# In the attentions of a two-layer decoder, ScalarE copies a finished group's output ahead of that step's transposed probabilities

## The chip, the cores and the metric

The kernel runs on one core of one Trainium2 chip. The metric is the device time of one execution in microseconds (us), as the median of several runs. The core's engines are TensorE (PE in the profile; its weight loads are PEld), VectorE (DVE), ScalarE (ACT), GpSimd (POOL) and SyncE (SP). Each works through its own list of instructions in order, and they wait for each other on semaphores.

## The reference, cut to what matters

The program computes two decoder layers over 64 sequences of 128 tokens and 256 features. Layer 0 is a gated delta-rule recurrence, a cross attention with tanh projections, and a mixture of four experts. Layer 1 is a causal attention with one shared head of keys and values, a causal cross attention, and a mixture of eight experts. The change concerns the three softmax attentions, each with 16 heads of 16 features:

```python
scores = jnp.einsum('bqhd,bkhd->bhqk', qh, kh) * scale
attn = jax.nn.softmax(scores, axis=-1)
ctx = jnp.einsum('bhqk,bkhd->bqhd', attn, vh).reshape(b, s, D)
return ctx @ Wo + bo
```

The two attentions of layer 1 add a causal mask to the scores.

## The kernel before

The 64 sequences are taken four at a time: one iteration handles G = 4 sequences, and a hardware loop runs 16 iterations. Each iteration runs the delta rule, attention 0, mixture 0, attention 1, attention 2 and mixture 1. No scheduler is involved: every engine has its own list, written by hand, and the order of the code is the order on the engine.

**An attention** (`attention(a_no)` exists once on PE, once on ACT, once on DVE) works on 16 "quads" (`QUADS`): a quad is four heads of one sequence, so four quads make one sequence, here called a group. The three copies of the loop run over steps `u` from 0 to 23, and each engine does in step u the work of several quads at different stages:

- PE multiplies queries by keys for two quads (L1076, in even steps; in attentions 1 and 2 two further matmuls add the mask, L1082); transposes the probabilities of quad u-3 into bank 3 or 4 (L1090, signals `t_psum`); multiplies values by the transposed probabilities of quad u-4 into bank 5 (L1102, signals `pv`). One step after a group's copy-out it transposes the group's output (L1111, `otr_psum`), and a step later the normalised output (L1132). From step 20 on it multiplies by the output weights (L1124).
- DVE takes each quad's row maximum (L1775) and subtracts it (L1779, `s_sub`). Per group it divides the output by the sum (L1793 reciprocal, L1795 product, `o_norm`).
- ACT exponentiates quad u-2 (L739 in attention 0, L737 in the others, `p_exp`), copies the transposed probabilities of quad u-3 from PSUM to SBUF (L746, waits for `t_psum`, signals `pt`), and per group copies the finished output from bank 5 (L750, waits for `pv`, signals `o_sb`) and later the transposed normalised output (L754).

**The wait around bank 5.** All four quads of a group write quarters of bank 5. So before the first quad of the next group (quads 4, 8 and 12, in steps 8, 12 and 16) PE waits:

```python
if v % 4 == 0 and g > 0:
    pe.wait_ge(S["o_sb"], at(it, "o_sb", a_no * G + g))
```

ACT makes that copy (L750) in the same steps 8, 12, 16 and, for the last group, 20. Step 20 has no copy of probabilities.

**GpSimd beside the attentions.** From mixture 0 on POOL runs a long serial chain of small additions for the next iteration's decay gates (`chain_links`, `chain_products`, L567), started by the gate weights of mixture 0 (`g_w`, DVE L1891). It ends with `au` (L610, `au_ready`) and goes on with `centered(it, 1)`, whose last operation is a subtraction over the whole 128x1024 tile `x_in` (L501). DVE uses `au` inside attention 2: before the division of group 2 it runs parts 0 to 4 of `decay_exponential` (17 dependent small steps, L1474 to L1493, the first of which waits for `au_ready`), and before that of group 3 parts 5 to 9 (17 more, L1492 to L1510):

```python
if a_no == 2 and b >= 2:
    for part in range(5 * (b - 2), 5 * (b - 1)):
        decay_exponential(part)
```

Of the kernel before, what the change touches and what calls it, by code (L numbers as in the profile page):

```python
# [13 lines left out]
ACT = mybir.ActivationFunctionType  # L14
# [8 lines left out]
G = 4  # L23
# [4 lines left out]
QUADS = G * NH // QH  # L28
# [43 lines left out]
def decoder_kernel(nc, a, out):  # L72
# [7 lines left out]
    with ExitStack() as ctx:  # L80
# [3 lines left out]
        def sem(name):  # L84
            return ctx.enter_context(nc.semaphore(name))
# [59 lines left out]
        def cut(first, *shape):  # L145

            size = 1
            for n in shape:
                size *= n
            flat = arena[:, first * G * D:first * G * D + size]  # L150
            names = "abcde"[:len(shape)]
            return flat.rearrange(f"p ({' '.join(names)}) -> p {' '.join(names)}", **dict(zip(names, shape)))
# [53 lines left out]
        osb = cut(10, 2, N)  # L206
# [54 lines left out]
        bank = [ctx.enter_context(nc.psum_tensor(f"bank{n}", [P, 512], F32)) for n in range(8)]  # L261

        S = {name: sem(name) for name in PER}
# [6 lines left out]
        def nth(it, per, n, ahead=0):  # L270

            return it * per + (ahead * per + n)

        def at(it, name, n):

            assert n > 0
            return nth(it, PER[name], n)
# [340 lines left out]
        def _(act):  # L618
# [61 lines left out]
            with nc.Fori(0, NIT, engines=[act.engine], hint_back_edge=True) as it:  # L680
# [48 lines left out]
                def attention(a_no):  # L729
                    for u in range(QUADS + 8):  # L730
                        if u >= 2 and u - 2 < QUADS:
                            v = u - 2
                            act.wait_ge(S["s_sub"], at(it, "s_sub", a_no * QUADS + v + 1))
                            if a_no > 0:
                                if v == 0:
                                    act.wait_ge(S["hl_fix"], at(it, "hl_fix", 6 * (a_no + 2) + 6))
                                act.activation(Ssb[:, v % 4], Ssb[:, v % 4], ACT.Exp, scale=rstd[:, v // 4:v // 4 + 1]).then_inc(S["p_exp"], 1)  # L737
                            else:
                                act.activation(Ssb[:, v % 4], Ssb[:, v % 4], ACT.Exp, scale=SCALE).then_inc(S["p_exp"], 1)  # L739
                        if u >= 3 and u - 3 < QUADS:  # L740
                            v = u - 3
                            act.wait_ge(S["t_psum"], at(it, "t_psum", a_no * QUADS + v + 1))
                            if v >= 2:

                                act.wait_ge(S["pv"], at(it, "pv", a_no * QUADS + v - 1))
                            act.activation(PT[:, v % 2], bank[3 + v % 2][:, :].rearrange("p (h q) -> p h q", h=QH), ACT.Copy).then_inc(S["pt"], 1)  # L746
                        if u >= 5 and (u - 5) % 4 == 3 and (u - 5) // 4 < G:
                            b = (u - 5) // 4
                            act.wait_ge(S["pv"], at(it, "pv", a_no * QUADS + 4 * b + 4))
                            act.activation(osb[:, b % 2, :], bank[5][:, :], ACT.Copy).then_inc(S["o_sb"], 1)  # L750
                        if u >= 7 and (u - 7) % 4 == 3 and (u - 7) // 4 < G:
                            b = (u - 7) // 4
                            act.wait_ge(S["attT_psum"], at(it, "attT_psum", a_no * G + b + 1))
                            act.activation(attT[:, :, b * P:(b + 1) * P],  # L754
                                           bank[7][:, 0:C * P].rearrange("p (c t) -> p c t", c=C), ACT.Copy).then_inc(S["attT"], 1)
# [28 lines left out]
                for c in range(C):  # L784
                    key_masks(0, c, bank[6 + c], True)
                act.preload_act_table_set(LN_EXP_TABLE)
                attention(0)


# [33 lines left out]
                act.activation(latT, bank[2][:, :], ACT.Copy).then_inc(S["lat"], 1)  # L823
                latent_masks()
                attention(1)


                key_masks(2, 0, bank[2], False)
                xT_copy(4)
                key_masks(2, 1, bank[3], False)  # L830
                half_rstd(4)
                attention(2)


# [1219 lines left out]
```

## Time and profile before

| | us |
|---|---|
| median of 3 runs | 5632.31 (5630.9 to 5637.03) |
| profiled execution, whole | 5640.22 |
| its span | 5637.7 |
| PE busy | 4736.9 (84%) |
| DVE busy | 4265.8 (76%) |
| POOL busy | 3826.9 (68%) |
| ACT busy | 2325.5 (41%) |

Busy time is the sum over an engine's instructions, and the span runs from the first to the last of them. The chain that ended last puts 58% of the span on PE, 23% on DVE and 8% on ACT. TensorE's granted clock is near full after the first slices. One iteration takes about 331 us, and the three attentions lie at 389 to 426, 516 to 556 and 568 to 609 us in the first.

### The profile page before, as it was taken

Reading aid. Unit: us, or ns where it says so; the run is one execution under the profiler, and the core shown is the slowest. Engines: PE = TensorE matmul, PEld = TensorE weight load, DVE = VectorE, ACT = ScalarE, POOL = GpSimd, SP = SyncE. Lnnn points to the kernel's source line nnn. Section 1 sums busy time; section 2 is a strip of 40 time slices with the busy share of each in tenths; the row PEclk is TensorE's granted clock in tenths of the full one; section 3 lists DMA queues with packets and bytes.
Section 4 is the critical chain, followed back from the end, with each engine's and each line's share of the span. In section 5 each row is a group of like instructions: output and inputs, shape, how many; then the busy total and the mean of one; then the engine's idle time right before and its main releaser. Section 6 shows DMA issues by size and latency. Waiting matters only on the chain.

```text
span 5637.7 us, 105981 instructions
## 1 busy us (share of the span) xinstructions
PE 4736.9 (84%) x28362; PEld 3112.3 (55%) x28362; DVE 4265.8 (76%) x11558; ACT 2325.5 (41%) x4480; POOL 3826.9 (68%) x10625
## 2 busy tenths in 40 slices
PE   1069898888889889888988988898898889889888
PEld 0045655656566465655646565565656556565655
DVE  5868777777777778777777878777787877778777
ACT  0034344444334444444444444444443444444344
POOL 1158676785867678586767858676785867768585
PEclk7589999999999999999999999999999999999999
DMA  3000000000000000000000000000000000000000
GB/s 85 8 12 1 28 1 13 16 9 20 1 24 5 11 18 9 20 1 24 5 9 20 9 20 1 24 5 9 20 5 24 1 24 5 9 20 1 20 1 16
DMA packets 61879, 78.07 MB, mean 14 GB/s; under 512 B 11168, under 2 KB 53808, under 8 KB 61232
## 3 DMA queue, kind: packets, MB, share of 16 engines
q1 hardware_dynamic: 52784, 62.42, 3.4%
q10 hardware_dynamic: 8448, 8.39, 0.4%
q8 instruction: 240, 3.93, 0.3%
q14 instruction: 407, 3.33, 0.2%
HBM read 45.04 MB, written 8.46 MB: 9 GB/s over the span
## 4 chain that ended last, share of the span: by engine, by line
PE 58%; DVE 23%; issue 8%; ACT 8%; POOL 1%; SPq 1%; DMA 1%; DVEq 0%; ACTq 0%; POOLq 0%
PE bank L1171 8%; PE bank L1090 6%; PE bank L1204 5%; PE bank L1076 5%; PE bank L1102 4%; PE bank L1000 3%; PE bank L1124 3%; PE bank L1007 3%; PE bank L1189 2%; PE bank L1111 2%; DVE arena L2004 2%; PE bank L1082 2%; ACT arena L763 2%; ACT arena L750 1%; PE bank L1132 1%
## 5 line engine op out<-in xcount | busy, mean ns | idle before, releaser
L746 ACT ACTIVATE arena<-bank 128x512 f32<-128x512 f32 x768 | 454.4, 592 | 386.9 <-PE bank L1090 386.9
L1775 DVE TENSOR_REDUCE smax<-bank 128x4 f32<-128x512 f32 x768 | 525.5, 684 | 114.6 <-PE bank L1082 66.1
L1779 DVE TENSOR_TENSOR arena<-bank,smax 128x512 f32<-128x512 f32 x768 | 531.2, 692 | 26.4
L1090 PE MATMUL bank<-ident,arena 128*128 128x128 f32 x3072 | 489.4, 282 | 46.9 <-ACT arena L737 29.2
L1171 PE MATMUL bank<-w,arena 128*128 128x512 f32 x1024 | 482.2, 601 | 14.0 <-DVE arena L1727 14.0
L1102 PE MATMUL bank<-arena 128*32 128x128 f32 x6144 | 329.1, 286 | 192.3 <-ACT arena L750 192.3
L1076 PE MATMUL bank<-arena 64*128 64x512 f32 x1536 | 436.4, 645 | 64.4 <-ACT arena L774 28.0
L1090 PEld LDWEIGHTS bank<-ident,arena 128*128 128x128 f32 x3072 | 348.7, 142 | 247.8 <-ACT arena L739 83.0
L1204 PE MATMUL bank<-w,arena 128*128 128x256 f32 x2048 | 454.1, 380 | 13.9 <-ACT arena L809 13.9
L737 ACT ACTIVATE arena<-arena,rstd 128x512 f32<-128x512 f32 x512 | 368.2, 719 | 203.4 <-DVE arena L1779 197.5
L1204 PEld LDWEIGHTS bank<-w,arena 128*128 128x128 f32 x2048 | 387.8, 190 | 90.3 <-issue 23.0
L567 POOL TENSOR_TENSOR acc_a<-acc_s,arena 128x32 f32<-128x32 f32 x1008 | 262.7, 261 | 204.2 <-DVE gate L1891 80.5
L501 POOL TENSOR_TENSOR arena<-arena 128x1024 f32<-128x1024 f32 x17 | 32.2, 1896 | 517.1 <-DVE y_nat L1559 517.0
L809 ACT ACTIVATE arena<-bank,lnb,lng 128x512 f32<-128x512 f32 x256 | 197.1, 776 | 407.2 <-PE bank L1189 404.5
L567 POOL TENSOR_TENSOR acc_c<-acc_a,acc_b 128x32 f32<-128x32 f32 x1008 | 267.1, 265 | 79.7
L567 POOL TENSOR_TENSOR acc_s<-acc_a,acc_c 128x32 f32<-128x32 f32 x1008 | 265.3, 263 | 78.9
L567 POOL TENSOR_TENSOR acc_c<-acc_c,arena 128x32 f32<-128x32 f32 x1008 | 265.0, 263 | 78.9
L567 POOL TENSOR_TENSOR acc_b<-acc_a,acc_s 128x32 f32<-128x32 f32 x1008 | 264.3, 262 | 78.8
L567 POOL TENSOR_TENSOR acc_c<-acc_c,acc_d 128x32 f32<-128x32 f32 x1008 | 261.9, 260 | 78.9
L882 PE MATMUL bank<-causal,identb 128*128 128x512 bf16 x658 | 164.2, 390 | 173.6 <-DVE y_nat L1559 166.5
L1102 PEld LDWEIGHTS bank<-arena 128*32 128x32 f32 x6144 | 125.4, 108 | 328.5 <-ACT arena L746 238.6
L567 POOL TENSOR_TENSOR arena<-arena,sl_t 128x256 f32<-128x256 f32 x384 | 287.5, 749 | 27.6
(428 smaller groups left out, 11948.0 us busy)
## 6 DMA issues: line engine op xcount, KB each, us to landing
arena<-in_x_dram SPq DMA_DIRECT2D x35, 512.0 KB, 3.5
xn_next<-arena SPq DMA_DIRECT2D x17, 512.0 KB, 2.9
arena<-cum_dram SPq DMA_DIRECT2D x17, 512.0 KB, 3.7
arena<-in_ctx_dram SPq DMA_DIRECT2D x16, 512.0 KB, 3.5
out_dram<-arena ACTq DMA_DIRECT2D x16, 512.0 KB, 3.1
xn<-xn_next SPq DMA_DIRECT2D x15, 512.0 KB, 2.9
w<-in_L_ffn_w_dram SPq DMA_DIRECT2D x8, 512.0 KB
w<-in_L_ffn_w_dram SPq DMA_DIRECT2D x1, 1024.0 KB
```

What stands on the lines that cost most here:

```text
L567: operation(*operands).then_inc(chain_step, 1)
L737: act.activation(Ssb[:, v % 4], Ssb[:, v % 4], ACT.Exp, scale=rstd[:, v // 4:v // 4 + 1]).then_inc(S["p_exp"], 1)
L746: act.activation(PT[:, v % 2], bank[3 + v % 2][:, :].rearrange("p (h q) -> p h q", h=QH), ACT.Copy).then_inc(S["pt"], 1)
L809: act.activation(zT[:, e % 2, k, :], bank[4 + n % 2][:, :], ACT.Relu, scale=lng[:, e, k:k + 1], bias=lnb[:, e, k:k + 1]).then_inc(S["zT"], 1)
L1000: ins = mm(bank[2 + h][:, sl], lev[:, l % 2, h, sl], Tm[:, h, sl], start=True, stop=True)
L1076: ins = mm(bank[S_BANKS[v % 4]][:, :], QT[rows, c, g * P:(g + 1) * P], KM[rows, g, min(c, chunks - 1)].rearrange("p h t -> p (h t)"), star ...
L1090: ins = tr(bank[3 + v % 2][:, j * P:(j + 1) * P], Ssb[:, v % 4, j, :], ident[:, :])
L1102: ins = mm(bank[5][2 * HD * j:2 * HD * (j + 1), (v % 4) * P:(v % 4 + 1) * P], V2[:, g, (v % 4) * QH + j, :], PT[:, v % 2, j, :], start=Tru ...
L1171: ins = mm(bank[g][:, :], xT[:, c, g * P:(g + 1) * P], w1_0[:, e, c, :], start=(c == 0), stop=(c == C - 1))
L1204: ins = mm(bank[6 + g // 2][:, (g % 2) * D:(g % 2 + 1) * D], zT[:, e % 2, k, g * P:(g + 1) * P], w2_0[:, e, k, :], start=(k == 0), stop=(k ...
L1775: dve.tensor_reduce(smax[:, u, :], sc, AX, ALU.max).then_inc(S["s_max"], 1)
L1779: dve.tensor_tensor(Ssb[:, u % 4], sc, smax[:, u, :].unsqueeze(2).broadcast_to([P, QH, P]), ALU.subtract).then_inc(S["s_sub"], 1)
```

## The change

In ACT's list the copy of a finished group's output is written ahead of the copy of transposed probabilities of the same step, instead of behind it. Nothing is added or removed, and the lists of PE, DVE, POOL and SP stay as they are.

```diff
                                 act.activation(Ssb[:, v % 4], Ssb[:, v % 4], ACT.Exp, scale=SCALE).then_inc(S["p_exp"], 1)
+                        if u >= 5 and (u - 5) % 4 == 3 and (u - 5) // 4 < G:
+                            b = (u - 5) // 4
+                            act.wait_ge(S["pv"], at(it, "pv", a_no * QUADS + 4 * b + 4))
+                            act.activation(osb[:, b % 2, :], bank[5][:, :], ACT.Copy).then_inc(S["o_sb"], 1)
                         if u >= 3 and u - 3 < QUADS:
                             v = u - 3
                             act.wait_ge(S["t_psum"], at(it, "t_psum", a_no * QUADS + v + 1))
...
                             act.activation(PT[:, v % 2], bank[3 + v % 2][:, :].rearrange("p (h q) -> p h q", h=QH), ACT.Copy).then_inc(S["pt"], 1)
-                        if u >= 5 and (u - 5) % 4 == 3 and (u - 5) // 4 < G:
-                            b = (u - 5) // 4
-                            act.wait_ge(S["pv"], at(it, "pv", a_no * QUADS + 4 * b + 4))
-                            act.activation(osb[:, b % 2, :], bank[5][:, :], ACT.Copy).then_inc(S["o_sb"], 1)
```

On ACT in attention 0, steps 8 and 9, stand before: exponential of quad 6 (L739), probabilities of quad 5 (L746), output of group 0 (L750), a register instruction, exponential of quad 7, probabilities of quad 6.

```order
L739 ACTIVATE arena<-arena 128x512
L746 ACTIVATE arena<-bank 128x512
L750 ACTIVATE arena<-bank 128x512
L733 REGISTER_ALU
L739 ACTIVATE arena<-arena 128x512
L746 ACTIVATE arena<-bank 128x512
```

At the same place now the output copy has line 743 and the copy of probabilities line 750.

```order
L739 ACTIVATE arena<-arena 128x512
L743 ACTIVATE arena<-bank 128x512
L750 ACTIVATE arena<-bank 128x512
L733 REGISTER_ALU
L739 ACTIVATE arena<-arena 128x512
L750 ACTIVATE arena<-bank 128x512
```

The output of group 0 has changed places with the probabilities of quad 5. The second place is ACT's steps 10 to 12 of attention 0, from the copy of group 0's normalised output (L754) to the copies of step 12, before:

```order
L754 ACTIVATE arena<-bank 128x2x128
L733 REGISTER_ALU
L739 ACTIVATE arena<-arena 128x512
L746 ACTIVATE arena<-bank 128x512
L733 REGISTER_ALU
L739 ACTIVATE arena<-arena 128x512
L746 ACTIVATE arena<-bank 128x512
L750 ACTIVATE arena<-bank 128x512
```

And the same steps now:

```order
L754 ACTIVATE arena<-bank 128x2x128
L733 REGISTER_ALU
L739 ACTIVATE arena<-arena 128x512
L750 ACTIVATE arena<-bank 128x512
L733 REGISTER_ALU
L739 ACTIVATE arena<-arena 128x512
L743 ACTIVATE arena<-bank 128x512
L750 ACTIVATE arena<-bank 128x512
```

Group 1's output now comes right behind the exponential of quad 10, with the copy of quad 9's probabilities behind it; between L754 and that exponential nothing moved. Steps 14 to 16 differ in the same way, and so do the other two attentions. In step 20 nothing moves. That is three moves in each of three attentions in each of 16 iterations: 144.

## Rows read from the trace of the kernel before

**Rows 1.** Groups by line, whole run: busy us, mean ns of one; idle before, releasers.

```profile
L1779 DVE TENSOR_TENSOR arena<-bank,smax 128x512 f32<-128x512 f32 x768 | 531.2, 692 | 26.4
L1775 DVE TENSOR_REDUCE smax<-bank 128x4 f32<-128x512 f32 x768 | 525.5, 684 | 114.6 <-PE bank L1082 66.1 <-PE bank L1076 36.9
...
L1102 PE MATMUL bank<-arena 128*32 128x128 f32 x6144 | 329.1, 286 | 192.3 <-ACT arena L750 192.3
```

**Rows 2.** Timeline of PE, attention 0, iteration 0: start us, length us, instruction.

```profile
398.78 0.43 PE L1102 MATMUL bank<-arena 128*32 128x128 f32 x8
...
402.12 0.42 PE L1102 MATMUL bank<-arena 128*32 128x128 f32 x8 [1.27 <-ACT arena L750]
...
410.15 0.43 PE L1102 MATMUL bank<-arena 128*32 128x128 f32 x8 [1.27 <-ACT arena L750]
...
417.53 0.43 PE L1102 MATMUL bank<-arena 128*32 128x128 f32 x8 [1.41 <-ACT arena L750]
```

**Rows 3.** Timeline of ACT in the same attention.

```profile
399.50 0.63 ACT L739 ACTIVATE arena<-arena 128x512 f32<-128x512 f32 x1
400.89 0.60 ACT L746 ACTIVATE arena<-bank 128x512 f32<-128x512 f32 x1 [0.77 <-PE bank L1090]
401.39 0.59 ACT L750 ACTIVATE arena<-bank 128x512 f32<-128x512 f32 x1
...
406.48 0.38 ACT L754 ACTIVATE arena<-bank 128x256 f32<-128x256 f32 x1
406.76 0.62 ACT L739 ACTIVATE arena<-arena 128x512 f32<-128x512 f32 x1
407.28 0.59 ACT L746 ACTIVATE arena<-bank 128x512 f32<-128x512 f32 x1
407.76 0.63 ACT L739 ACTIVATE arena<-arena 128x512 f32<-128x512 f32 x1
...
414.51 0.38 ACT L754 ACTIVATE arena<-bank 128x256 f32<-128x256 f32 x1
```

**Rows 4.** Timelines of PE and ACT, attention 1, iteration 0, step 8.

```profile
530.98 0.43 PE L1102 MATMUL bank<-arena 128*32 128x128 f32 x8 [1.27 <-ACT arena L750]
...
529.13 0.72 ACT L737 ACTIVATE arena<-arena,rstd 128x512 f32<-128x512 f32 x1 [0.80 <-DVE arena L1779]
```

**Rows 5.** Timeline of POOL, iteration 0: the chain's start, its end, and `centered`'s last operation.

```profile
448.38 0.25 POOL L567 TENSOR_TENSOR acc_a<-acc_s,arena 128x32 f32<-128x32 f32 x1 [4.83 <-DVE gate L1891]
...
593.51 0.20 POOL L610 TENSOR_TENSOR au<-acc_a 128x8 f32<-128x8 f32 x1
...
601.21 1.89 POOL L501 TENSOR_TENSOR arena<-arena,row 128x1024 f32<-128x1024 f32 x1
```

**Rows 6.** Timeline of DVE, attention 2, iteration 0: first decay step, group 2's reciprocal, step 18, group 3's reciprocal.

```profile
597.40 0.18 DVE L1474 TENSOR_TENSOR dec_t<-au,a_row 128x8 f32<-128x8 f32 x1
...
601.39 0.26 DVE L1793 RECIPROCAL orec<-bank 128x16 f32<-128x16 f32 x1 [0.47 <-PE bank L1111]
...
602.02 1.10 DVE L1492 TENSOR_TENSOR dec_t<-dec_t 128x10 f32<-128x10 f32 x1
...
606.45 0.26 DVE L1793 RECIPROCAL orec<-bank 128x16 f32<-128x16 f32 x1
```

**Rows 7.** Timeline of PE there: group 3's transpose of the normalised output.

```profile
607.23 0.44 PE L1132 MATMUL bank<-ident,arena 128*128 128x128 f32 x2 [1.91 <-DVE arena L1795]
```

**Rows 8.** Timelines of POOL and DVE at the same places of iteration 4.

```profile
1926.34 0.20 POOL L610 TENSOR_TENSOR au<-acc_a 128x8 f32<-128x8 f32 x1
...
1934.09 1.89 POOL L501 TENSOR_TENSOR arena<-arena,row 128x1024 f32<-128x1024 f32 x1
...
1928.55 0.28 DVE L1474 TENSOR_TENSOR dec_t<-au,a_row 128x8 f32<-128x8 f32 x1
...
1934.20 1.82 DVE L1496 TENSOR_TENSOR dec_t<-dec_t 128x10 f32<-128x10 f32 x1
...
1938.31 0.26 DVE L1793 RECIPROCAL orec<-bank 128x16 f32<-128x16 f32 x1
```

## The prediction

> **What bounds the kernel now.** I began with the groups by line. PE's products of values and probabilities (L1102) have 192.3 us of idle time in front of them, and all of it is put down to ACT's copy L750, the one that moves [rows 1]. That is 3.4% of the span, in 144 waits of 1.34 us on average: three per attention, the three places where bank 5 changes groups. Next I read PE's timeline of one attention, to see whether these waits stand alone. They nearly do: in attention 0 PE has 1.27 us of idle time before each of the first two and 1.41 us before the third, and hardly any elsewhere [rows 2]. The pattern repeats in each iteration to 0.03 us. DVE is not the bound of attention 0: it takes 684 and 692 ns per quad [rows 1], 5.5 us per group of four, plus 0.7 us for the division, 6.2 us, where PE takes 410.15 - 402.12 = 8.03 us with its wait and 6.76 without [rows 2].
>
> ACT's timeline shows what stands in the wait [rows 3]. In step 8 the exponential of quad 6 starts at 399.50. ACT then waits 0.77 us for PE's transposes of quad 5, copies them at 400.89, and only then, at 401.39, copies group 0's output, which PE had finished writing at 399.21 [rows 2]. PE goes on at 402.12, 0.73 us after the start of that copy.
>
> So in attention 0 the path runs: PE transposes quad 5, ACT copies them, ACT copies the output, PE multiplies. The change cuts the first two links out.
>
> **The change at each of the three places.** Nothing is added or removed. 144 copies of 0.60 us change places with 144 copies of 0.60 us, so ACT's busy time stays. What matters is when each of the two can start.
>
> *First wait (step 8), attention 0.* After the exponential at 399.50 the next ACT instruction can start 0.52 us later (as 406.76 to 407.28 in [rows 3]), at 400.02. The output has been there since 399.21, so the copy starts at 400.02 and PE could go on at 400.02 + 0.73 = 400.75. PE itself is free at 402.12 - 1.27 = 400.85 [rows 2]. The wait is gone: 1.3 us. The copy of quad 5's probabilities is not delayed, since its transposes arrive at 400.89 and ACT is free at 400.5.
>
> *Second wait (step 12).* Here ACT has a queue. Behind the copy L754 of the normalised output come the exponential of quad 9, the copy of quad 8, the exponential of quad 10, then now the output copy. From L754 to the copy of quad 8 is 0.80 us (406.48 to 407.28), to the next exponential 0.48 (407.76), then 0.52 to the output copy, 0.73 to PE: 2.53 us from the start of L754. Before, it was 410.15 - 406.48 = 3.67 [rows 2, 3]. The difference is 1.14 us, under PE's 1.27, so a wait of some 0.1 us stays.
>
> *Third wait (step 16).* The same ladder of 2.53 us starts at L754 of group 1; before, it was 417.53 - 414.51 = 3.02 [rows 2, 3]. Only 0.49 us is won, because there PE had been fast and ACT is the late one: 0.9 us of the 1.41 remains.
>
> Attention 0 gains 1.33 + 1.14 + 0.49 = 2.96 us. Its end is set by PE, and mixture 0 waits for it.
>
> *Attention 1.* In step 8 DVE is late: the exponential waits for it until 529.13 and takes 0.72 us instead of 0.63 [rows 4]. The output copy can start about 0.61 later, at 529.74, and PE at 530.47 instead of 530.98: 0.5 us. The second wait can go whole, but for some 0.1 us that DVE's division then delays PE: 1.2. The third again 0.5. Sum 2.2 us.
>
> *Attention 2.* DVE is not late in step 8, so 1.3 + 1.3 before the scores of the last quads, and 0.5 after: 3.1 us.
>
> Taken alone, that is 2.96 + 2.2 + 3.1 = 8.3 us per iteration, 132 in all.
>
> **What is late next.** At the end of attention 2 DVE needs `au` from POOL. POOL's chain starts with mixture 0's gates and takes 593.51 - 448.38 = 145.13 us [rows 5]; over the 16 iterations it is 144.7 to 145.2. It doesn't depend on the attentions. The gain in attention 0 lies ahead of its start (POOL waits 4.83 us there [rows 5], so it starts earlier by the full 2.96). The gains of attentions 1 and 2 lie beside it. DVE asks for `au` at 597.40 [rows 6], 3.69 us after its end at 593.71. In iteration 4 it asks at 1928.55, 2.01 us after 1926.54 [rows 8]. Seven iterations are like the first (3.4 to 3.9 us), seven like iteration 4 (2.0), two have over 8. The change would bring DVE there 2.2 + 2.6 = 4.8 us earlier, so in 14 iterations it will wait for POOL, and POOL's `au` sets the end of attention 2.
>
> From there on I count from A, the start of `au`. DVE's first decay step would start at about A + 0.3 (0.20 for `au`, 0.1 taken for the signal). A step takes 0.206 us: 16 of them fill 603.12 to 606.45 [rows 6], less a gap of 0.04. The 17 steps ahead of group 2's reciprocal take 3.5. The reciprocal and the product take 602.02 - 601.39 = 0.63, with no wait left for PE, and the next 17 steps 3.5. Group 3's reciprocal would be due at A + 7.9, its last decay step starting at A + 7.7.
>
> At A + 7.70 (iteration 0 [rows 5]) or A + 7.75 (iteration 4 [rows 8]) POOL starts its 1.89 us subtraction over x_in. What such a meeting does can be read: the decay step that starts during it lasts 1.10 us in iteration 0 and 1.82 in iteration 4 in place of 0.17, and ends within 0.03 us of POOL's end [rows 5, 6, 8]. A reciprocal from PSUM at 601.39, inside the same operation, was not held. So the last step, if it starts after POOL's, is held to A + 9.6, and group 3's reciprocal comes at A + 9.65. I take it as held; the margin is 0.05 us either way.
>
> The page SBUF — State Buffer of the Trainium skill (Who interferes with whom) gives the rule for such a pair: a VectorE instruction with two SBUF inputs and a GpSimd instruction that reads SBUF share a port, and whichever starts first has it for its whole length. By that rule the outcome hangs on the order of two starts alone; a last step that came first would hold POOL for 0.2 us and would itself not be held. The rows agree as far as POOL comes first.
>
> PE's wait of 1.91 us [rows 7] says that this reciprocal, and not PE, ends attention 2 today. Before it came at 606.45 = A + 12.94, in iteration 4 at 1938.31 = A + 11.97 [rows 6, 8]. So attentions 1 and 2 together gain 12.94 - 9.65 = 3.3 us in seven iterations, 11.97 - 9.65 = 2.3 in seven, and about 4.6 in the two with slack.
>
> **The sum.** Attention 0: 16 x 2.96 = 47. Attentions 1 and 2: 7 x 3.3 + 7 x 2.3 + 2 x 4.6 = 48. Together 95 to 96 us. The profiled execution took 5640.2 (span 5637.7 and 2.5 around it), so 5544; the median of the runs is 7.9 lower, and I forecast 5536, 1.7% less. Its own range is 5526 to 5548: each gain in attention 0 is known to 0.2 us.
>
> **Rivals.**
>
> *The last decay step slips in ahead of POOL's subtraction.* Then the reciprocal comes at A + 7.9 to 8.0 and 14 iterations gain 1.7 us more: 23 less, 5513. For it: the margin above. Against it: the 0.1 us for the signal is a guess, and a longer one makes the step later.
>
> *POOL doesn't hold DVE back.* Its chain would have to shorten with the attentions. The full 132 would give 5500. The constancy of 145 us speaks against it.
>
> *The later waits come back.* If only the first wait of each attention shrinks, because ACT's queue in steps 12 and 16 is longer than my ladder, the gain is 1.3 + 0.5 + 1.3, and 0.5 of DVE's wait for PE at 601.39 [rows 6]: 3.6 x 16 = 58, 5574.
>
> *Nothing comes of it.* Mixture 0 and mixture 1 could be held by something that doesn't move. PE works gapless into mixture 0, which speaks against it; 5632.
>
> *Slower.* The output copy now stands ahead of the copy of probabilities and waits for `pv`. If the group's last products were late, ACT would stand there with transposes already finished, and PE with its next products and transposes behind both. The price is up to 0.48 us for each of 144, 69 us: 5701. It begins where `pv` of the old group comes later than the transposes of the new one. PE issues them in the opposite order, and the margin in step 8 is 400.89 - 399.21 = 1.7 us [rows 2, 3].
>
> **Chances.** Forecast 0.42; last step slips in 0.25; POOL no bound 0.06; waits come back 0.15; nothing 0.06; slower 0.06. From the slipped step to the returning waits is 0.82 plus what lies between, so the range is 5505 to 5574. A measurement of this kernel can tell 0.2%, 11 us, from no change. Faster by more than that 0.91, within it 0.05, slower 0.04.
>
> **What the profile will show.** PE's idle time before L1102 put down to the output copy should fall from 192.3 us to 30 to 60, nearly all in the third waits of about 0.9 us. ACT's output copy should start right behind the exponential, and the copy of probabilities in step 8 where it did, 0.69 us after its transposes. DVE should show a new wait for POOL's `au` at L1474, in 14 iterations, 1 to 3 us long. One late decay step per iteration should last 1.9 us, and group 3's reciprocal should start 9.65 us after `au`; 7.9 would mean that the step slipped in. The forecast is wrong if the first waits stay over 0.3 us, if POOL's chain takes other than 145 us, or if the mixtures get longer by what the attentions lose.

## The result, and the profile after

| | before | after |
|---|---|---|
| median of the timed runs (4 each) | 5634.01 us (5630.9 to 5637.03) | 5584.52 us (5573.22 to 5593.83) |
| profiled execution, and its span | 5640.22, 5637.7 us | 5573.22, 5571.5 us |
| mean granted clock of the profiled execution | 0.950 | 0.950 |

The ratio is 0.9909, with a 95% interval of 0.9892 to 0.9925. The kernel is 49.5 us faster. The forecast was 5536 us, 96 less than the 5632.31 that stood as the median then, and 5584.5 lies above the range, which ended at 5574. In the two profiled executions the difference is 67 us; but the profiled execution of the kernel before lies above all of its timed runs, and that of the changed kernel is its fastest. One execution of one kernel below (e6), 6836.98 us long at a mean clock of 0.674, is left out of that kernel's median.

The attentions did what was forecast. This is the line of PE's products in the groups by line of the changed kernel, and then its line and DVE's new one in the chain of waits (us in total, times, longest). ACT's copy of the output is L743 now and the copy of probabilities L750.

```profile
L1102 PE MATMUL bank<-arena 128*32 128x128 f32 x6144 | 329.6, 286 | 60.4 <-ACT arena L743 58.2
```
```profile
PE bank L1102 <- ACT arena L743: 58.2, 64, 1.0
POOL acc_a L567 <- DVE gate L1891: 46.9, 16, 2.9
DVE dec_t L1474 <- POOL au L610: 39.5, 15, 3.2
```

192.3 us of waiting [rows 1] became 58.2, in 64 waits where there were 144: per iteration one in attention 0, two in attention 1 and one in attention 2. In ACT's timeline of attention 0, iteration 0, the output copy starts behind the exponential and the copy of probabilities where it did. Beside it stand PE's rows around the first place, and the one wait that is left, at the third:

```profile
399.75 0.63 ACT L739 ACTIVATE arena<-arena 128x512 f32<-128x512 f32 x1
400.29 0.58 ACT L743 ACTIVATE arena<-bank 128x512 f32<-128x512 f32 x1
401.16 0.60 ACT L750 ACTIVATE arena<-bank 128x512 f32<-128x512 f32 x1 [0.30 <-PE bank L1090]
```
```profile
400.47 0.66 PE L1090 MATMUL bank<-ident,arena 128*128 128x128 f32 x4
401.05 0.43 PE L1102 MATMUL bank<-arena 128*32 128x128 f32 x8
401.41 0.66 PE L1090 MATMUL bank<-ident,arena 128*128 128x128 f32 x4
...
414.86 0.42 PE L1102 MATMUL bank<-arena 128*32 128x128 f32 x8 [0.93 <-ACT arena L743]
```

From its first scores (L1076) to its first residual addition (L1799) attention 0 takes 31.68 us in place of 34.62, 2.94 less; attention 1 takes 35.2 in place of 37.4, 2.2 less.

The end of attention 2 also went as forecast. The timelines of POOL, DVE and PE in iteration 5 (the rows answer to [rows 5 to 8]):

```profile
2231.66 0.20 POOL L610 TENSOR_TENSOR au<-acc_a 128x8 f32<-128x8 f32 x1
...
2239.47 1.91 POOL L501 TENSOR_TENSOR arena<-arena,row 128x1024 f32<-128x1024 f32 x1
```
```profile
2231.89 0.26 DVE L1474 TENSOR_TENSOR dec_t<-au,a_row 128x8 f32<-128x8 f32 x1 [3.22 <-POOL au L610]
...
2239.45 0.17 DVE L1509 TENSOR_TENSOR dec_t<-dec_t 128x10 f32<-128x10 f32 x1
2239.66 1.75 DVE L1510 TENSOR_TENSOR dec_t<-dec_t 128x10 f32<-128x10 f32 x1
2241.44 0.26 DVE L1793 RECIPROCAL orec<-bank 128x16 f32<-128x16 f32 x1
```
```profile
2236.27 0.69 PE L1132 MATMUL bank<-ident,arena 128*128 128x128 f32 x2 [3.50 <-DVE arena L1795]
2239.34 0.75 PE L1111 MATMUL bank<-ident,arena 128*128 128x128 f32 x4
```

DVE waits 3.22 us for `au`, the last decay step starts 0.19 us behind POOL's subtraction and is held to its end, and group 3's reciprocal comes 9.78 us after `au` (forecast 9.65). In 15 of the 16 iterations it comes 9.77 to 9.80 us after `au`; iteration 12, where DVE is late by itself, has 11.39.

Then where did the gain go? I put the same marks into the timelines of both kernels and took the mean of each part over 15 iterations, in us. A residual addition is DVE's L1799, of which each attention has two; 2.04 us between the first two stay as they are:

| part | before | after | difference |
|---|---|---|---|
| first scores to first residual addition | 34.81 | 31.68 | -3.13 |
| second residual addition to `gate` (L1891) | 22.43 | 23.65 | +1.22 |
| `gate` to `au`, POOL's chain | 145.28 | 145.89 | +0.61 |
| `au` to the fifth residual addition | 13.44 | 10.52 | -2.92 |
| from there to the next iteration's first scores | 113.67 | 113.96 | +0.29 |
| iteration | 331.66 | 327.73 | -3.93 |

The rows of -3.13 and -2.92 are the forecast's two gains, 6.05 together where it had 6.0. The other three give 2.1 back, 34 us in 16 iterations. (The -3.13 is 2.94 of the attention itself; in two iterations before, attention 0 also had a stretch at the lower clock and took 36.07 us.)

*The +1.22.* These are POOL and DVE in iteration 0, before and then after:

```profile
441.21 2.34 POOL L595 TENSOR_TENSOR arena<-arena,onb_row 128x1024 f32<-128x1024 f32 x1
...
442.21 1.38 DVE L1828 TENSOR_TENSOR r_lg<-r_raw,gmx 128x16 f32<-128x16 f32 x1
445.31 0.18 DVE L1845 TENSOR_TENSOR arena<-arena,lt_mask 128x16 f32<-128x16 f32 x1
```
```profile
441.62 2.35 POOL L595 TENSOR_TENSOR arena<-arena,onb_row 128x1024 f32<-128x1024 f32 x1
446.90 0.25 POOL L567 TENSOR_TENSOR acc_a<-acc_s,arena 128x32 f32<-128x32 f32 x1 [2.93 <-DVE gate L1891]
...
441.73 2.28 DVE L1845 TENSOR_TENSOR arena<-arena,lt_mask 128x16 f32<-128x16 f32 x1
446.57 0.17 DVE L1891 TENSOR_TENSOR gate<-gtop,grc 128x16 f32<-128x16 f32 x1
```

POOL's addition of a bias row ends work that did not move with attention 0: it starts at 441.62 where it started at 441.21. DVE's steps of the gates now come some three microseconds earlier against it. Before, the addition already held one of them, L1828, for 1.38 us in place of 0.17 (in 13 of 15 iterations; in the other two it held a neighbour for 1.6). That step now comes ahead of it and takes 0.18, and another one, L1845, starts 0.11 us behind the addition and takes 2.28 us instead of 0.18, in all 15. So one meeting was exchanged for a longer one, which costs 0.90 us net, and several of the 0.17 us steps around it now take 0.23 to 0.27, which makes up the other 0.3. POOL's own wait for the gates shrinks by 1.90 us, not by 2.96.

*The +0.61.* POOL has no wait between `gate` and `au`, before or after. Its 390 operations there are busy for 125.94 us before and 126.59 after (means of 15 iterations), and the gaps between them are the same. So the time lies in the length of single operations. Most additions of the chain take 0.25 us, and some take up to 0.78 while DVE combines two tiles. The same holding runs here in the other direction, as in these rows of DVE and POOL from the changed kernel, in which DVE started 0.04 us ahead:

```profile
2111.28 0.69 DVE L1444 TENSOR_TENSOR arena<-arena 128x512 f32<-128x512 f32 x1
```
```profile
2111.32 0.76 POOL L567 TENSOR_TENSOR acc_c<-acc_s,acc_c 128x32 f32<-128x32 f32 x1
```

Before, the addition at this place took 0.25 us, and others were held instead. Why the sum comes out 0.65 larger is not settled.

*The +0.29.* It is the mean of a gain and a loss: 1.2 us less from the fifth residual addition to the delta rule's start (L1998), 1.5 us more from there on. The granted clock tells them apart. Windows of 2 us around the end of PE's wait of 3.50 us above, in iteration 5 (busy us of each engine, granted clock, DMA share):

```profile
2234.00:2236.00 2.00, 0.00 (x0) 0.00 (x0) 1.69 (x10) 0.00 (x0) 1.61 (x6) 1.00 0.00 0
2236.00:2238.00 2.00, 1.73 (x11) 1.00 (x12) 1.73 (x10) 0.77 (x2) 1.61 (x6) 0.56 0.00 0
2238.00:2240.00 2.00, 2.00 (x9) 1.56 (x8) 1.73 (x9) 0.21 (x1) 1.61 (x6) 0.59 0.00 0
2240.00:2242.00 2.00, 0.96 (x5) 0.50 (x4) 1.93 (x3) 0.00 (x0) 1.38 (x1) 1.00 0.00 0
```

For 3.4 us TensorE had its lower level, 1.2 instead of 2.4 GHz. Read in windows of 1 us over the whole trace, both kernels are full of such stretches, most of them 3.4 or 6.8 us long and a few from 10 to 17.1. From 300 us on they make some 330 us before and 321 after, of which 32 are the end of the program's start, ahead of the first attention. What changed is their places. In iteration 4 they start, in us from the iteration's first scores, at 217, 228 and 272 before, and at 207, 224, 245 and 269 after. What one costs can be read in mixture 1, over the same 100 rows of PE: iteration 1 before has no stretch there, iteration 5 after has the one at 245, and PE is busy for 19.73 and 21.71 us. Windows before, then after:

```profile
968.00:989.00 21.00, 19.73 (x100) 16.44 (x98) 18.72 (x41) 4.68 (x5) 16.09 (x31) 1.00 0.14 52
```
```profile
2270.00:2293.00 23.00, 21.71 (x100) 17.59 (x98) 19.12 (x41) 4.68 (x5) 16.44 (x31) 0.93 0.15 48
```

*The rest of the difference.* 3.93 us in each of 16 iterations is 63 of the profiles' 67 us. The timed runs give less, 49.5. Some 6 us of that are the kernel before, whose profiled execution took 5640.22 where its timed runs have a median of 5634.01. The other 11 are the changed kernel: the profiled execution was the fastest of the four, at a clock of 0.950; the other three had 0.938 to 0.943 and took 5583.8 to 5593.8. They have no trace, so that the stretches at half clock made them longer is likely and not shown.

### The profile page after: what moved, and what is told of

Its sections match the earlier page's. It is cut to its first block, busy times and chain, and to the rows that moved or that the text cites. A ratio compares the mean times of both kernels' runs of the same rounds, so it can differ in the third digit from the quotient of the medians.

```text
span 5571.5 us, 105820 instructions
## 1 busy us (share of the span) xinstructions
PE 4721.9 (85%) x28201; PEld 3108.1 (56%) x28362; DVE 4301.8 (77%) x11558; ACT 2322.5 (42%) x4480; POOL 3843.9 (69%) x10625
## 3 DMA queue, kind: packets, MB, share of 16 engines
q8 instruction: 240, 3.93, 0.3%
## 4 chain that ended last, share of the span: by engine, by line
POOL 32%; PE 27%; DVE 22%; issue 12%; ACT 4%; POOLq 3%; SPq 1%; DMA 0%; DVEq 0%; ACTq 0%
POOL acc_c L567 12%; POOL arena L567 6%; PE bank L1000 3%; POOL acc_b L567 3%; POOL acc_a L567 3%; POOL acc_s L567 3%; PE bank L1007 3%; POOL sl_t L567 3%; POOLq L566 3%; PE bank L1171 2%; DVE arena L2004 2%; PE bank L1090 2%; PE bank L1124 2%; ACT arena L763 2%; PE bank L1076 1%
## 5 line engine op out<-in xcount | busy, mean ns | idle before, releaser
L750 ACT ACTIVATE arena<-bank 128x512 f32<-128x512 f32 x768 | 454.8, 592 | 244.0 <-PE bank L1090 237.9
L1076 PE MATMUL bank<-arena 64*128 64x512 f32 x1536 | 434.5, 642 | 64.6 <-ACT arena L774 28.0
L1204 PEld LDWEIGHTS bank<-w,arena 128*128 128x128 f32 x2048 | 387.8, 190 | 90.3 <-issue 23.0
L1102 PE MATMUL bank<-arena 128*32 128x128 f32 x6144 | 329.6, 286 | 60.4 <-ACT arena L743 58.2
L579 POOL TENSOR_TENSOR arena<-arena,levmask 128x512 f32<-128x512 f32 x192 | 262.2, 1387 | 57.6 <-DVE arena L1602 42.9
L1171 PEld LDWEIGHTS bank<-w,arena 128*128 128x128 f32 x1024 | 179.7, 192 | 164.3 <-issue 147.0
```

The costliest lines, as they stand in the source:

```text
L579: pool.tensor_tensor(heads(lev[:, l % 2, h, :]), heads(MT[:, h, :]), levmask[:, l, :].unsqueeze(1).broadcast_to([P, G, P]), ALU.mult).then ...
L1076: ins = mm(bank[S_BANKS[v % 4]][:, :], QT[rows, c, g * P:(g + 1) * P], KM[rows, g, min(c, chunks - 1)].rearrange("p h t -> p (h t)"), star ...
L1102: ins = mm(bank[5][2 * HD * j:2 * HD * (j + 1), (v % 4) * P:(v % 4 + 1) * P], V2[:, g, (v % 4) * QH + j, :], PT[:, v % 2, j, :], start=Tru ...
L1171: ins = mm(bank[g][:, :], xT[:, c, g * P:(g + 1) * P], w1_0[:, e, c, :], start=(c == 0), stop=(c == C - 1))
L1204: ins = mm(bank[6 + g // 2][:, (g % 2) * D:(g % 2 + 1) * D], zT[:, e % 2, k, g * P:(g + 1) * P], w2_0[:, e, k, :], start=(k == 0), stop=(k ...
```

## The experiments

"Half clock" is worked out from the profile's granted clock, as the sum over windows of 1 us of 2 x (1 - clock), from 300 us on (so each sum has some 30 us of the start in it). "The part up to `gate`" and the like are the rows of the table above, as means of 15 iterations. Medians and ratios are against the kernel before on the same chip in the same session. That kernel's own median was 5644.18 beside e1 to e4, 5694.29 beside e5 to e8, and 5688.22 beside e9 to e12, so kernels of one session are what to compare. e1 to e4 and e9 to e12 ran on one chip and e5 to e8 on another, and even on the one chip that kernel's median moved by 44 us, at mean clocks from 0.952 down to 0.937. A ratio to it carries this too: it makes a kernel of a later session look better than one of the first.

### The changed kernel again

> The changed kernel once more. Theory: its median is held down by two things that its first profile shows, GpSimd's fixed chain and half-clock stretches of TensorE whose number differs from run to run. Expected ratio 0.987 to 0.993, with a spread between runs over 8 us, and a lower mean granted clock in the slower runs. Rival (the first four runs were a bad draw): 0.984 and a spread like the kernel before, 6 us.

5580.54 us against 5644.18, ratio 0.9878 (0.9853 to 0.9904). Both kernels have runs of several lengths. The kernel before ran from 5630.95 at a clock of 0.952 to 5672.19 at 0.946. In its second profile the parts are the same to 0.06 us. The expectation held: the ratio lies within it, and the runs spread over 9.7 us. The slower runs have the lower clock only roughly (5572.08 and 5581.28 us both have 0.944). So I take it that a difference of two medians here carries some 10 to 15 us that is not the edit's.

### One half at a time

```diff
- if u >= 5 and (u - 5) % 4 == 3 and (u - 5) // 4 < G:
+ if u >= 5 and (u - 5) % 4 == 3 and (u - 5) // 4 < G and a_no in (0,):
      ... (ahead of the copy of probabilities)
+ the same copy behind it, with a_no not in (0,)
```

For the second kernel `in` and `not in` change places.

> The copy goes first in attention 0 alone. Theory: the attention itself gets 2.94 us shorter per iteration, but GpSimd's 2.3 us addition of the bias row, which doesn't move with it, now lands on the gates and gives 1.2 us of it back: 1.7 x 16 = 27 us, ratio 0.995. Rival (the loss in mixture 0 comes from elsewhere, or from all three attentions): 2.9 x 16 = 47 us, ratio 0.992.

> The copy goes first in attentions 1 and 2 alone. Theory: DVE waits for au at the end of attention 2 in most iterations and the gain there is 2.2 to 3.2 us per iteration, less what longer half-clock stretches in mixture 1 take: 20 to 50 us, ratio 0.991 to 0.996; together with the run of attention 0 alone it should add up to the whole within 10 us. Rival (GpSimd's chain doesn't bind without the move in attention 0, since it would start later): no wait for au, 5.3 x 16 = 85 us, ratio 0.985.

Attention 0 alone: 5628.85 us, ratio 0.9971 (0.9948 to 0.9994), 15 us. Attentions 1 and 2 alone: 5610.45, ratio 0.9937 (0.989 to 0.9983), 34 us. Together that is 49, where the whole change has 64 and I had expected agreement within 10; the intervals are wide enough for both. Attention 0 alone also falls short of the 27 us expected.

Attention 0 alone shows its 2.94 us gained in all iterations, and the part up to `gate` at 23.66 against 22.43, exactly the loss of the whole change, with L1845 at 2.28 us in every iteration. So the longer hold belongs to attention 0's gain. With the other half alone that part is 22.60. Of what is left of attention 0's gain, 1.7 us per iteration, most goes as well: 0.6 into POOL's chain, and 0.9 behind `au`, where attentions 1 and 2 arrive later. In iteration 4 a stretch at half clock starts at 156, in attention 1, which takes 38.77 us where it took 37.44. This stretch, at 156 to 158, is in 13 of 15 iterations and was in two before. The mean iteration is 331.1 us, and was 331.7.

The other half shows the stretches at their longest. DVE waits for `au` in only 6 iterations of its profile, where I had expected most. Its runs spread from 5572.13 us to 5652.1, at clocks from 0.951 to 0.931, and the profiled one is among the long. Its windows in iteration 4, from the end of mixture 0 into attention 1 (first scores at 1848), with half clock through 17 us:

```profile
1835.00:1838.00 3.00, 1.92 (x4) 0.82 (x4) 2.74 (x16) 1.47 (x5) 2.45 (x10) 0.81 0.02 5
1838.00:1841.00 3.00, 2.31 (x8) 1.09 (x6) 0.47 (x3) 0.60 (x1) 2.38 (x10) 0.50 0.00 0
1841.00:1844.00 3.00, 3.00 (x7) 1.79 (x8) 0.96 (x2) 0.00 (x0) 2.38 (x11) 0.50 0.01 3
...
1850.00:1853.00 3.00, 3.00 (x9) 0.66 (x8) 2.27 (x4) 0.72 (x1) 2.38 (x11) 0.50 0.00 0
1853.00:1856.00 3.00, 2.84 (x14) 1.41 (x14) 2.81 (x6) 1.96 (x3) 2.43 (x10) 0.84 0.00 0
```

PE's timeline ahead of it has two waits of 1.0 and 1.1 us within three microseconds:

```profile
1834.42 0.66 PE L957 MATMUL bank<-ident,arena 128*128 128x128 f32 x4 [1.02 <-DVE arena L1906]
1836.16 1.36 PE L1218 MATMUL bank<-arena,Wcd 128*128 128x512 f32 x2 [1.08 <-DVE arena L1731]
```

Half clock is 499 us in this execution, and its mean iteration, 331.9 us, is no shorter than before; its fastest run, 5572.13, has the whole change's time. Of the first seven iterations those with the 17 us stretch take 332.7 to 334.7 us, those with only 3.4 us there 331.0.

### The bias row ahead of the chain

```diff
  (POOL)
- chain_links(pool, link, 1, 0, ROUTER_LINKS)
+ chain_links(pool, link, 1, 0, 1)
      ... (wait for hl_mean, addition of the bias row)
+ chain_links(pool, link, 1, 1, ROUTER_LINKS)
```

> The changed kernel, with GpSimd's addition of the bias row moved four links earlier in its chain, to where DVE reads PSUM. Theory: the gate step that took 2.28 us takes 0.17 again, the stretch from the second residual addition to the gates falls from 23.65 to 21.4 to 22.4 us, and the iteration gets 1.2 to 2.2 us shorter: 20 to 35 us less than the changed kernel. Rival (the gates end by something else): the same time as the changed kernel.

5570.76 us, ratio 0.9864 (0.9837 to 0.9891), 10 us under the changed kernel in the same session, with overlapping ranges, where I had expected 20 to 35. The mechanism is confirmed: L1845 no longer takes 2.28 us, and the part up to `gate` is 22.37 in place of 23.66. It is not free of holds, though. The addition, at its new place, now holds another DVE step (L1669 of this kernel, 0.75 to 0.81 us), and the same move in the kernel before (e8 below, which has a second one too) brings the part down to 21.28.

The iteration got shorter by only 0.1 to 0.2 us. Mixture 0 (from `gate` to attention 1's first scores) took 69.41 in place of 67.60 and brought a new stretch at half clock in six of the first seven iterations, 50 us after the first scores; half clock rose from 321 to 376. But mixture 0 lies beside POOL's chain, and there it mostly used up DVE's wait for `au`, which fell from 3.2 us in most iterations to 1.1 or less. What is lost for the time lies behind the fifth residual addition: 115.05 us in place of 113.96. There most iterations have 6.8 us of half clock at 221, where the changed kernel has 3.4 at 225.

### Dummy matmuls into the long wait of attention 2

```diff
+ if a_no == 2 and u >= 18:
+     keep_busy(12 if u == 18 else 4, 2)
```

> The changed kernel, with 12 and 4 dummy bf16 matmuls ahead of the last two transposes of normalised output in attention 2, where PE idles 3.5 and 1.25 us. They take about 0.21 us each and add nothing to the path as long as PE would wait anyway. Theory (TensorE's half clock after that wait costs time in mixture 1): the half-clock stretch that begins there disappears, the granted clock's mean rises, and 1 to 2 us per iteration come back, 15 to 35 us. Rival (the clock there costs nothing, since DVE sets the end of attention 2 and of mixture 1): the same time as the changed kernel within 8 us.

5576.27 us against 5694.29, ratio 0.9798 (0.9777 to 0.9818). The changed kernel itself did not run beside it. Its time elsewhere is 5580.54, and e5's profile has its parts (iteration 327.84 and 327.77 us), so I take the two as equal, and the expected 15 to 35 us less did not come. Against the kernel before e5 looks 118 us better because that one is slower there than beside e1 to e4. The stretch at 207 is gone in the first seven iterations, so that wait had to do with it. In iteration 4 others start at 49, 117, 223, 247 and 267, and half clock is 388, more than without these matmuls.

### The late decay steps behind the attention

```diff
  (DVE)
- if a_no == 2 and b >= 2:
-     for part in range(5 * (b - 2), 5 * (b - 1)):
+ if a_no == 2 and b == 3:
+     for part in range(5):
          decay_exponential(part)
      ...
+ for part in range(5, 10):        (behind xT_copy(5))
+     decay_exponential(part)
```

> The changed kernel, with DVE's ten parts of the decay exponential taken off the path: five behind the wait of group 2's division, five behind the last copy ahead of the router of mixture 1, where DVE idles 2 to 4 us. Theory (GpSimd's au bounds the end of attention 2): the last scores to the first residual addition take 7 to 9 us from au in place of 10.4, DVE's wait for au falls below 1 us, 20 to 40 us less than the changed kernel. Rival (PE would bind there at once): the same time.

> The changed kernel with the bias row added early and the decay steps late. If the two terms are apart, the gains of the two runs add up: 30 to 60 us less than the changed kernel, near 5530. If TensorE's half-clock stretches take what is given, it stays above 5555.

> The kernel before with the same two moves and without the change. It shows what the moves are worth by themselves: with the old order GpSimd doesn't bind (DVE asks for au 2.0 to 3.7 us late) and the gates meet the bias row only in part, so I expect 0 to 25 us less than the kernel before, and the changed order on top of the moves to be worth 80 to 120 us, the 5.9 us of PE's waits in attentions 0 to 2 undiminished.

The late steps bring the changed kernel to 5520.21 us, ratio 0.9699 (0.9679 to 0.9719). That is about 56 us under e5, which has the changed kernel's parts, and more than the 20 to 40 expected. From `au` to the fifth residual addition it takes 5.7 to 7.5 us in 12 of 15 iterations, in place of 10.4, and DVE never waits for `au`. The other three iterations take 12.1 to 12.9 there, behind stretches at half clock of 10 and 17 us. So `au` and the two halves of decay steps behind it were what ended attention 2.

With the bias row moved too it is 5547.62 us (0.9748, 0.9728 to 0.9768), 27 more, so the two gains don't add up. The part up to `gate` is short again (22.36), POOL's chain and the rest of the iteration give back 1.0 us of that, and the part behind `au` takes 1.5 us more (9.11 and 7.58). Half clock is 408 against 350.

The same two moves on the kernel before give 5694.37 us, ratio 1.0 (0.9983 to 1.0017). Its part up to `gate` is 21.28, 1.15 us less than in the profile before, which fits the hold that this kernel had there already. Nothing comes of it: eight of 15 iterations have a 17.1 us stretch at half clock and take 337.8 us each, and half clock is 488. Whether the moves brought these stretches is open, since the kernel before ran at about the same clock beside them (0.934 to 0.945) and has no profile from there. In the company of these two moves the change is worth 147 us (80 to 120 expected). The 50 to 64 us of the change alone come from sessions in which the kernel before was 50 to 60 us faster than here, so 147 is no measure of what the moves add.

### Work in TensorE's waits, in both kernels

The same dummy matmuls (`keep_busy(n, bank)`: n products of a 128x128 by a 128x512 tile in bf16, whose results nobody reads) go into five places where PE waits, in the kernel before (e9), the changed one (e10), with the late decay steps (e11) and with both moves (e12).

```diff
+ keep_busy((5, 8)[h], h)      (layer 0, ahead of inv_eye)
      ...
- keep_busy(8, 4)
+ keep_busy(16, 4)             (ahead of mixture 0's experts)
      ...
+ keep_busy(4, 6)              (ahead of xT_ready(3))
      ...
+ keep_busy(3, 6)              (ahead of k_rows)
      ...
+ keep_busy(5, 6)              (ahead of attention(1))
```

> The kernel before, with dummy bf16 matmuls in the waits of PE that its half-clock stretches follow: 8 more ahead of mixture 0's first transposes (wait 2.2 us), 4, 3 and 5 ahead of attention 1 (0.7 to 1.75 us each), 5 and 8 at the start of the delta rule (1.2 and 1.9 us). They lengthen nothing by themselves. Theory (half-clock stretches cost time on PE's path): the stretches at 52, at 118 to 121 and at 270 us of an iteration shrink or go, the mean clock rises by 0.01 or more, 20 to 60 us less than the kernel before on the same chip. Rival (they lie beside other engines' work): no difference.

> The changed kernel with the same dummy matmuls. Theory (with the clock held up, the change is worth what its waits say, less GpSimd's share): ratio to the same fills without the change 0.982 to 0.986, that is 80 to 100 us, near the 96 predicted. Rival (the missing half of the gain isn't in the clock): 40 to 65 us, as between the two kernels without fills.

> The changed kernel with the decay steps late and the same dummy matmuls. 50 to 60 us below the changed kernel with the fills if au is a term of its own; 5460 to 5500 us.

> Decay steps late, bias row early, and the same dummy matmuls. Theory (the early bias row failed to pay only through the clock): 15 to 30 us below the run with the decay steps late and fills. Rival: the same.

| kernel | median us | ratio to before | half clock us | mean clock |
|---|---|---|---|---|
| e9, before + filling | 5631.97 | 0.9907 (0.9885 to 0.9929) | 234 | 0.958 |
| e10, changed + filling | 5527.38 | 0.9723 (0.97 to 0.9745) | 208 | 0.960 |
| e11, e10 + late decay steps | 5469.36 | 0.962 (0.9598 to 0.9641) | 147 | 0.965 |
| e12, e11 + bias row early | 5468.49 | 0.9619 (0.9597 to 0.9641) | 186 | 0.962 |

Matmuls that compute nothing took 56 us off the kernel before, within the 20 to 60 expected: it ran at 5647.64 to 5696.57 beside them, e9 at 5630.23 to 5633.58. In the first sessions the kernel before had single runs as fast as that, 5630.9 and 5630.95. So the filling took away the long stretches and the spread, and did not beat the kernel's best. For the changed kernel it did: e10 has 5522.5 to 5530.58, and that kernel's fastest run without filling is 5572.08. e10's windows at the same place of iteration 4, where e3 had 17 us at half clock:

```profile
1807.00:1810.00 3.00, 2.31 (x11) 1.11 (x9) 1.72 (x12) 1.10 (x3) 2.45 (x12) 1.00 0.00 0
1810.00:1813.00 3.00, 3.00 (x15) 1.64 (x15) 2.20 (x4) 0.00 (x0) 2.39 (x10) 1.00 0.01 3
1813.00:1816.00 3.00, 2.42 (x13) 0.80 (x11) 1.89 (x7) 2.73 (x8) 2.44 (x10) 1.00 0.00 0
```

Between e9 and e10 the change is worth 104.6 us, with both far narrower than that, and more than the 80 to 100 expected. Part by part and per iteration the difference is -3.60 in attention 0, +0.96 to `gate`, -0.04 in POOL's chain, -2.42 behind `au`, and -1.69 in what follows. The hold is still there; the +0.61 of the chain and the +0.29 of the rest are not. Of the -3.60, 0.66 is a stretch near 29 that e9 has in its attention 0, and the -1.69 goes with stretches that e10 has not or has elsewhere. These two are 38 of the 105 us: the places of half clock once more, in this change's favour here. Without them some 67 us are left. That 105 comes near the 96 forecast is luck.

In e11's DVE timeline, iteration 4, group 2 no longer waits for `au`, and group 3's reciprocal comes 5.45 us after `au` started (1880.56), ahead of POOL's subtraction:

```profile
1881.70 0.26 DVE L1797 RECIPROCAL orec<-bank 128x16 f32<-128x16 f32 x1 [3.35 <-PE bank L1112]
1881.99 0.42 DVE L1799 TENSOR_TENSOR arena<-bank,orec 128x256 f32<-128x256 f32 x1
1882.33 0.32 DVE L1478 TENSOR_TENSOR dec_t<-au,a_row 128x8 f32<-128x8 f32 x1
...
1886.01 0.26 DVE L1797 RECIPROCAL orec<-bank 128x16 f32<-128x16 f32 x1
```

e11 lies 58 us under e10, as expected. e11 and e12 are the best versions, 3.8% below the kernel before in their session and 2.9% below its first median. e12 misses its expected 15 to 30 us under e11. It has the shorter part up to `gate` (22.37 against 23.67), but POOL's chain to `au` takes 0.29 us more, the part behind it 0.33 more and the rest of the iteration 0.29 more, and half clock is 39 us longer. 0.4 us per iteration stays in the profile, and nothing in the medians.

## Why the prediction missed

**What held.** All three waits of each attention changed as worked out: 2.94 us for attention 0 (forecast 2.96), 2.2 for attention 1 (2.2), 58.2 us left of PE's waiting (30 to 60), the longest 1.0; some 11 of them are first waits of attention 1 (0.7 us), which the list of signs had not named. DVE waits for `au` in 15 iterations (14 forecast), by 0.9 to 3.2 us. `au` sets the end of attention 2: undoing what stands behind it (e6, e11) moves that end and the time. The last decay step is held, and the reciprocal comes at A + 9.78 (9.65). With a margin of 0.05 us on record this was a choice between two near outcomes, and that it fell right is luck in part: the step came 0.19 us behind POOL's. By the Trainium skill's page SBUF — State Buffer (Who interferes with whom) the order of the two starts decides who is held. The trace agrees, with POOL 0.19 us ahead here and 0.11 ahead of L1845, and with DVE 0.04 us ahead of the POOL addition that it held. None of the rivals is what happened as a whole: the "slower" one would show ACT waiting for PE's products at L743, and that wait is 2.5 us in the whole run. The nearest is "Nothing comes of it", which said that mixture 0 could be held by something that doesn't move. That came true for 1.22 us of 2.96, and I had set it aside because PE works gapless into mixture 0. Two of the signs of being wrong on record came too: the chain takes other than 145 us, and mixture 0 got longer by a part of what attention 0 lost.

**The first step that failed** is the sentence on attention 0, "Its end is set by PE, and mixture 0 waits for it", with its continuation that POOL's chain "starts earlier by the full 2.96". I followed PE into mixture 0 and did not ask what stands still beside a path that moves. POOL's 2.34 us addition (L595) stood still, DVE's gate steps moved against it, and 1.22 us of the 2.96 were lost: 20 us in 16 iterations. The trace before already showed the pair at work, in L1828's 1.38 us, so the question could have been asked. e2 shows that the loss comes with attention 0 alone, e4 that the 2.28 us go when the addition moves. I had applied this very rule to the end of attention 2 and to no other place.

**The second** is that the sum has no term for TensorE's clock. Every duration came from rows at whatever clock that row had. Iteration 3 of the kernel before, 9 us longer than its neighbours, has a 17.1 us stretch at half clock from the end of mixture 0 into attention 1, and my "seven and seven" iterations with 3.7 and 2.0 us of slack differ by where their stretches lie: each of the first seven has one at 52 (mixture 0, in five of them) or at 157 (attention 1, in two), and none of the other seven has. Mixture 0 up to attention 1's first scores is 1.9 us longer with the one at 52, and POOL's chain doesn't wait for it. I had used these patterns as if they belonged to the program. The change moves PE's waits and so moves the stretches; the part from the fifth residual addition to the next scores came out 0.29 us longer instead of the same. That is only 5 us here. In e4 and e8 a part got shorter by over 1 us and the iteration hardly or not at all, with more half clock elsewhere; and between e9 and e10, which hold their clock better, the change is worth 105 us, of which some 38 are again places of stretches.

**The third** is small. "The chain takes 145.13 us" and does not depend on the attentions. Counted from `gate` it took 145.28 us and takes 145.89 now, 0.61 more, 10 us in all. e9 and e10 have 145.77 and 145.72, so it is not the moved copy alone that lengthens it. POOL's operations are longer one by one, with no wait among them, and which DVE steps they meet differs from kernel to kernel. That this is the reason is likely and not shown.

In sum, from the profiles: 96 forecast, less 20 for the held gate step, 10 for POOL's chain, 5 for the rest of the iteration, makes 61, with 67 measured there. The missing 6 are what this account leaves over. The runs' median then gives 17 less than the profiles, as said above, and with it the miss is 46 us, of which the held gate steps are the one large piece that an experiment shows.

**Still open.** Why executions of one kernel differ in the number of stretches, and which wait sets off which, was not settled. The link between waits and stretches is shown only by adding matmuls in them (e5, e9 to e12). The places were not filled one at a time, and e5, which filled one, has more stretches elsewhere. Whether the kernel before would have had the stretches of e8 in that session was not looked at. What lengthens POOL's chain is open too.

## What to carry to other kernels

When a step moves earlier, list what does not move with it on the engines beside the path: a short operation of yours may now start just behind a long one of another engine, and it then pays for nearly the whole length of the long one. Look for such meetings in the trace before, too: one that is there already will move, and may get longer or shorter. Before costing a change, even in a kernel whose TensorE is 85% busy, read the granted clock in windows of a microsecond or two: rows from a stretch at half clock are not the program's, and a gain that only moves TensorE's waits may be taken back by such a stretch elsewhere. Compare two versions with the same filling in their waits if you want to know what the edit itself is worth, and only kernels of one session: the kernel before moved by 60 us between sessions.

## What I had not expected of the hardware

TensorE fell to its lower level for 3.4 us after waits as short as these: 3.50 us from 2232.8 in the changed kernel, and 1.02 and 1.08 us close together in e3, there for 17.1 us. In the kernel before no wait of PE from the first attention on is longer than 2.61 us, and it has such stretches in every iteration. From 300 us on they make 321 to 499 us at 1.2 GHz in kernels without filling, though TensorE is busy for 85% of the span, and 147 to 234 with it. And a DVE step of 0.18 us took 2.28 us beside a 2.35 us operation of POOL that had started 0.11 us before it.
